# The second layer's latent norm: which engine takes the sums of squares, in what order, and when the root runs

## The reference

```python
def rmsnorm(x, w):
    return x * jax.lax.rsqrt(jnp.mean(x * x, axis=-1, keepdims=True) + EPS) * w
...
q = rmsnorm(hidden_states @ wq_a.T, q_a_ln_w) @ wq_b.T        # 192 latents for the queries
...
ckv = hidden_states @ wkv_a.T
kv = rmsnorm(ckv[..., :KV_LORA], kv_a_ln_w)                   # 64 latents for keys and values
k_pe = ckv[..., KV_LORA:][:, None, :, :]                      # 64 rotary columns, not normed
...
x1 = _bitlinear(x, w1)
x2 = _bitlinear(x, w2)
hidden = jax.nn.sigmoid(x1) * x2                              # the second layer's feed-forward
return _bitlinear(hidden, w3)
```

## Time and profile before

| What | Value |
|---|---|
| median of 3 runs | 1327.66 us (1326.15 to 1327.93) |
| profiled execution, its own time | 1328.96 us |
| its span | 1327.2 us |
| mean granted clock of TensorE over the span | 0.938 |
| first batch's block (d1b0) | about 523 to 585 us |
| second batch's block (d1b1) | about 585 to 653 us |

### The profile page before, as it was taken

How to read it: one execution, slowest core, us unless ns; L and a number is a source line. 1 busy time by engine, 2 the same in 40 slices (tenths; PEclk the granted TensorE clock), 3 DMA queues, 4 the chain that set the end, 5 groups by cost and what they waited for, 6 DMA issues and landing times.

```text
span 1327.2 us, 22453 instructions
## 1 busy us (share of the span) xinstructions
PE 1200.7 (90%) x7552; PEld 856.9 (65%) x7552; DVE 896.5 (68%) x2308; ACT 751.5 (57%) x1700; POOL 547.1 (41%) x567
## 2 busy tenths in 40 slices
PE   4888779999999889887799999999999999999898
PEld 3776744444443477776567776777777777777688
DVE  6867587899997344444577666677766667777743
ACT  2466216677776424545466656666665566666632
POOL 2435233444441100607065554556655445565310
PEclk9898756899998797888899999999999999999999
DMA  6773154454540284021211111110111121011315
GB/s 187 147 147 59 45 73 58 59 80 81 76 64 3 68 236 137 31 85 48 76 29 44 45 45 43 30 33 29 44 45 45 49 87 33 29 45 33 128 38 185
DMA packets 112466, 93.55 MB, mean 70 GB/s; under 512 B 49696, under 2 KB 102240, under 8 KB 110560
## 3 DMA queue, kind: packets, MB, share of 16 engines
q1 hardware_dynamic: 112352, 92.11, 29.6%
HBM read 53.02 MB, written 30.67 MB: 63 GB/s over the span
## 4 chain that ended last, share of the span: by engine, by line
PE 35%; DVE 11%; issue 3%; ACT 1%; DMA 0%; ACTq 0%; DVEq 0%
PE psum L1025 11%; PE psum L1073 9%; PE psum L194 8%; PE psum L1046 7%; DVE a_part L938 3%; DVE psum L943 3%; DVE a_pt L976 2%; DVE w L2289 1%; ACT a_p L990 1%; DVE w_lat L2289 1%; DVE q00l L2289 1%; DVE q01l L2289 1%; DVE a_nm L943 1%; DMA w<-wf_d 0%; DVE ql1l L2170 0%
## 5 line engine op out<-in xcount | busy, mean ns | idle before, releaser
L1007 POOL TENSOR_SCALAR a_p<-a_p,a_rl 128x128 f32<-128x128 f32 (+7 forms) x256 | 218.8, 856 | 307.5 <-DVE a_rl L949 307.5
L990 ACT ACTIVATE a_p<-psum,a_nm 128x128 f32<-128x128 f32 (+7 forms) x256 | 189.7, 741 | 55.7 <-DVE a_nm L943 54.1
L1508 ACT ACTIVATE a_pt<-psum 128x512 f32<-128x512 f32 (+3 forms) x384 | 167.9, 492 | 80.0 <-PE psum L1371 77.5
L1046 PE MATMUL psum<-ident,a_p 128*128 128x128 f32 x1152 | 175.4, 279 | 14.2 <-DVE a_pt L976 14.2
L976 DVE COPY a_pt<-psum 128x512 f32<-128x512 f32 (+1 forms) x192 | 114.5, 596 | 109.0 <-PE psum L1046 108.5
L974 ACT ACTIVATE a_pt<-psum 128x256 f32<-128x256 f32 (+2 forms) x192 | 87.5, 456 | 164.0 <-PE psum L1046 163.9
L1046 PEld LDWEIGHTS psum<-ident,a_p 128*128 128x128 f32 x1152 | 127.2, 140 | 62.3 <-issue 47.7
L1073 PE MATMUL psum<-a_pt,v 128*64 128x256 f32 (+1 forms) x1280 | 159.4, 370 | 1.4 <-ACT rows_k L1087 1.4
L1361 PE MATMUL psum<-a_op_k,a_op_q 64*128 64x512 f32 (+3 forms) x384 | 137.4, 456 | 9.1 <-ACT a_op_q L1527 8.1
L1371 PE MATMUL psum<-a_op_q,a_op_k 64*128 64x512 f32 (+3 forms) x384 | 132.6, 432 | 7.5 <-ACT a_pt L1508 6.2
L1371 PEld LDWEIGHTS psum<-a_op_q,a_op_k 64*128 64x128 f32 x384 | 65.1, 201 | 104.4 <-ACT a_pt L1508 88.4
(11 more groups left out here) (389 smaller groups left out, 2907.7 us busy)
## 6 DMA issues: line engine op xcount, KB each, us to landing
ot_d<-rows_k SPq DMA_DIRECT2D x16, 512.0 KB, 4.5
a_swap<-w_p SPq DMA_DIRECT2D x60, 128.0 KB, 2.3
rows_q<-qk_d SPq DMA_DIRECT2D x48, 128.0 KB, 4.5
rows_k<-qk_d SPq DMA_DIRECT2D x48, 128.0 KB, 7.5
w<-wf_d SPq DMA_DIRECT2D x15, 384.0 KB, 3.4
qk_d<-d_stage_h SPq DMA_DIRECT2D x64, 64.0 KB, 2.1
qk_d<-d_stage_l SPq DMA_DIRECT2D x64, 64.0 KB, 2.1
d_x<-in_L_attn_x_dram SPq DMA_DIRECT2D x8, 256.0 KB, 7.2
```

The costliest lines, as they stand in the source:

```text
L990: e.activation(s.p[:, t % NPB, 0:(i + 1) * P], C.score[t % 2][:, 0:(i + 1) * P], ACT.Exp, scale=-1.0, bias=s.nm[:, k:k + 1], accum_out=s.l ...
L1007: e.tensor_scalar(s.p[:, t % NPB, 0:(i + 1) * P], s.p[:, t % NPB, 0:(i + 1) * P], s.rl[:, k:k + 1], 1.0, ALU.mult, ALU.mult).then_inc(s.no ...
L1046: ins = e.transpose(C.turn[par][:, (k - k0) * P:(k - k0 + 1) * P], s.p[:, tt % NPB, k * P:(k + 1) * P], C.ident[:, :])
L1508: e.activation(pt[:, k // G0 % NPT, hd, off:HALF], bank_b("score", g, k)[:, off:HALF], ACT.Exp, scale=-1.0).then_inc(exped, 1)
```

## The change

`project1` gets an argument `squares_on`. In the first batch ("scalar") ACT still takes the squares, but those of tile tt-1 directly behind the copy of tile tt, in the part `first`. In the second batch ("vector") DVE takes them, with `tensor_tensor_reduce` in the part `rest`. The root stays in `rest` on ACT, which has nothing else now, and in the second block `rest` moves ahead of `lifts`.

```diff
-def project1(ph, C, W, cos, sin, kv_ln, xt_h, xt_l, ql_h, ql_l, keys, v):
+def project1(ph, C, W, cos, sin, kv_ln, xt_h, xt_l, ql_h, ql_l, keys, v, squares_on):
...
             e.activation(lat[:, tt, :], banks[tt % 4][:, 0:LAT], ACT.Copy).then_inc(lat_out, 1)
+            if squares_on == "scalar" and tt >= 1:
+                act_squares(e, tt - 1)
+        if squares_on == "scalar":
+            act_squares(e, NT - 1)
+
+    def act_squares(e, tt):
+        e.wait_ge(lat_out, tt + 1)
+        for n, cols in enumerate((slice(0, QL), slice(QL, E))):
+            e.activation(junk[:, tt, cols], lat[:, tt, cols], ACT.Square, accum_out=ms[:, n, tt:tt + 1]).then_inc(ssq, 1)
+
+    def dve_squares(e, tt):
+        e.wait_ge(lat_out, tt + 1)
+        for n, cols in enumerate((slice(0, QL), slice(QL, E))):
+            e.tensor_tensor_reduce(out=junk[:, tt, cols], in0=lat[:, tt, cols], in1=lat[:, tt, cols], scale=1.0, scalar=0.0,
+                                   op0=ALU.mult, op1=ALU.add, accum_out=ms[:, n, tt:tt + 1]).then_inc(ssq, 1)
 
     def scalar(e):
-        for tt in range(NT):
-            e.wait_ge(lat_out, tt + 1)
-            e.activation(junk[:, tt, 0:QL], lat[:, tt, 0:QL], ACT.Square, accum_out=ms[:, 0, tt:tt + 1]).then_inc(ssq, 1)
-            e.activation(junk[:, tt, QL:E], lat[:, tt, QL:E], ACT.Square, accum_out=ms[:, 1, tt:tt + 1]).then_inc(ssq, 1)
         e.wait_ge(means, 2)
         e.activation(ms[:, :, :], ms[:, :, :], ACT.Sqrt).then_inc(root, 1)
 
     def vector(e):
+        if squares_on == "vector":
+            for tt in range(NT):
+                dve_squares(e, tt)
         e.wait_ge(ssq, 2 * NT)
...
-                        run(nc, load, first, lifts, load_x(xb[1], source[1], came), rest, rotation, f, rotated, turn1(ph.part("t1b1"), C, rest, f))
+                        run(nc, load, first, rest, lifts, load_x(xb[1], source[1], came), rotation, f, rotated, turn1(ph.part("t1b1"), C, rest, f))
```

More of the change, by code:

```diff
@@ L2556, in program @@
                         loads = [load_x(xb[b], source[b], came[b]) for b in (1, 0)]
-                        first, rest = project1(ph.part("p1b0"), C, W, cos, sin, kv_ln, *xt[0], *ql[0], keys[0], v[0])
+                        first, rest = project1(ph.part("p1b0"), C, W, cos, sin, kv_ln, *xt[0], *ql[0], keys[0], v[0], "scalar")
                         f = feed1(ph.part("f1b0"), C, W, rest, 0, *xt[0], xb[0], came[0], acc_d,
@@ L2563, in program @@
                     with Phase(nc, "d1b1") as ph:
-                        first, rest = project1(ph.part("p1b1"), C, W, cos, sin, kv_ln, *xt[1], *ql[1], keys[1], v[1])
+                        first, rest = project1(ph.part("p1b1"), C, W, cos, sin, kv_ln, *xt[1], *ql[1], keys[1], v[1], "vector")
                         came = [ph.sem(f"x{n}_came") for n in range(NT // 2)]
```

## The result

| | before | changed |
|---|---|---|
| median of 20 runs, us | 1325.88 (1315.76 to 1329.45) | 1316.86 (1309.64 to 1331.69) |
| ratio to before | | 0.994 [0.9915, 0.9965] |
| profiled execution, its span | 1327.2 | 1308.7 |

The account below looks back on a forecast made before the run. The prediction took PE's waits to bound the kernel, here feed-forward's first restart waiting for the gate of job 0. Second batch -8.2 and first +1.5 made -6.7, 1322.3 us, or 1321.0 as a median; range 1318.0 to 1325.0.

Parts of the forecast that it names:

- The median of the runs shown is 1327.66 us, 1.3 below that execution, and the prediction is for medians: 1321.0 us: Whole kernel: -6.7 from the profiled 1328.96 gives 1322.3; lowered by 1.3 to the median's level, 1321.0 us.
- 1 us of scatter between runs: Whole kernel: margin added to the full-blocking case to set the range's upper end, 1325.0 us.
- -8.2: Second batch, PE's restart: 4.8 squares, 1.5 table load and root, 2.0 clock, less 0.1 late; bounds -8.3 to -7.5.
- I take three hits, 1.3: First batch: line 256, moved later, meets POOL's products three times at up to 0.44 each; part of +1.5, bounds -0.1 to +3.7.
- two tiles fit between two turns of POOL: First batch, line 256 on DVE beside POOL's products: the reason given for taking three hits, 1.3 us.
- The rival of full blocking: First batch: POOL and line 256 block each other fully, +3.7; second -7.5; total 1323.9 us; chance 0.17.
- whose cold clock stays as it is: First batch: PE's restart comes later by +1.5, with its cold clock unchanged.
- No turns: First batch: DVE and POOL take no turns, +0.2, with -8.3 in the second; total 1319.6 us; chance 0.1.
- A switch of tables at twice its load: Second batch, ACT: table switches cost twice their load, PE restarts 2.1 us later than forecast; 1323.0 us; chance 0.02.
- Squares slow enough to hold the root: Second batch: DVE's squares delay root and query copies; at 2.5 us a tile 1335.4 us; chance 0.03.
- Nothing moves: Second block: another wait behind the gate held it to the same end; 1327.7 us; chance 0.04.
- theory (E): Set up after the measurement: what lies beyond the sum comes from the clock in code that the change does not touch.

Follow-up runs that it names:

- e3_rows_late: Changed kernel, but DVE scales the eight rows of line 256 only behind its product for job HT1 + 1: 1312.05 us, 0.991 of before.
- e8_rows_late_again: Repeat of `e3_rows_late` with no edit, beside the changed kernel on the same chip: 1306.22 us, 0.9848 of before.
- e7_change_again: Repeat of the changed kernel with no edit: 1315.98 us, 0.9918 of before.
- e4_order_before: Changed kernel, but `rest` back behind `lifts` in the second block, squares still on DVE: 1323.87 us, 1.0034 of before.
- e1_first_only: Changed kernel, but the second batch has its old squares and old order, so only the first batch's change remains: 1325.29 us, 1.002 of before.
- e5_act_squares: Changed kernel with its new order, but the second batch's squares on ACT between its copies, as in the first batch: 1318.79 us, 0.9944 of before.
- e2_second_only: Changed kernel, but the first batch has its old squares on ACT, so only the second batch's change remains: 1317.44 us, 0.9968 of before.
- e6_pool_held: Changed kernel, but in the first batch POOL's first product waits until line 256 is through: 1310.76 us, 0.9877 of before.

## Why the prediction was wrong in the number and right in the direction

The median, 1316.86 us, lies 1.1 us below the range of 1318.0 to 1325.0 and 4.1 below the forecast of 1321.0. The difference from before was forecast as -6.7; measured are -8.0 [-11.3, -4.6] by the ratio, and -7.3 by the blocks of the traces. The steps:

- **"The median of the runs shown is 1327.66 us, 1.3 below that execution, and the prediction is for medians: 1321.0 us", and in the range "1 us of scatter between runs". This step failed.** Three runs within 1.8 us had me take the base for fixed. In 20 runs beside the changed kernel the same program had 1325.88, in the 35 of the next comparison 1323.92, from 1312.51 to 1335.86. From 1325.88 the sum gives 1319.2 and the range 1316.2 to 1323.2, which holds the median; 1.8 of the 4.1 us are this step. The stretch ahead of the blocks alone took 507.5 to 523.4 us.
- **Second batch, "-8.2": the mechanism and its terms right, one term missing.** The gate 6.3 earlier (6.33), no wait of ACT for DVE, PE's wait at 0.37 (said 0.4), the restart at 2.4 GHz (said so), the last pair on DVE 0.55 (said near 0.7, at most 0.86), POOL's wait of 5.4 gone. The block became 9.8 shorter and not 8.2: in the traces of the change 1.5 more came from the warm start of the block, which the sum did not have. Where the start was cold, in `e3_rows_late`, the block became 7.1 shorter, since there the clock fell once more, to 0.57 between 44 and 48 us into the block. The six traces with the whole second part have blocks of 58.0 (three times), 60.6, 60.7 and 61.0, in the mean 59.4: that is 8.4 shorter than before, and so the 9.8 of the two traces of the changed kernel are partly luck with the clock.
- **"I take three hits, 1.3": mis-sized.** By its own terms the root of the first batch moved like this: line 256 starts 9.20 after the memset instead of 7.89 (+1.3, said +1.5), takes 5.55 instead of 3.11 (+2.4, said +1.3), the wait for the squares falls away (-1.3, as said), and the means take 0.77 instead of 0.25 (+0.5, counted within the three hits). The root comes 2.9 later, and in the mean of all traces 2.3, where +1.5 was said. My reason, that two tiles fit between two turns of POOL, was false: once both run together one tile goes to each product of POOL and nearly every tile takes 0.88. The rival of full blocking (+3.7) had the mechanism; in this trace it came to 2.9, with five more long tiles instead of six and one long mean instead of two.
- **"whose cold clock stays as it is": right**, 0.50 behind the restart in both.
- The other rivals. No turns: refuted by 5.55 against 2.67. A switch of tables at twice its load: refuted, the load of 584.24 takes 1.28 and the root starts at 585.53. The prediction put this rival outside its range, yet its 1323.0 us lie inside 1318.0 to 1325.0; the time alone would not have told it apart. Squares slow enough to hold the root: refuted, the pair takes 0.55 where 1.7 was needed. Nothing moves: refuted, -7.3 us in the blocks.
- The rule of the Trainium skill (Vector Engine (DVE) Microarchitecture Reference, section Points that are easy to get wrong) that two sources in SBUF that are not bf16 halve the throughput of this family: the trace disagrees. 192 columns from SBUF took 0.36 us, just what the row with one operand in PSUM had given for that length; the estimate by the rule was 1.1 us a tile. Both sources were the same tile, and two different ones were not run; whether the instruction is of the form that the page means, no row says.
- The rule of the Trainium skill (GPSIMD Engine Reference, section Specifications) on interfaces to SBUF shared with VectorE: the trace agrees that the two engines hold each other up, 0.88 us a tile beside POOL's products and 0.41 with POOL held. Whether line 256 meets the page's condition (a two-port mode or two inputs from SBUF) no run shows.

**What stays open.** The ratio gives 8.0 us and that of the repetition 10.9, the medians 9.0 and 9.5, the blocks of the two traces 7.3. All lie within both intervals (4.6 to 11.3 and, in the repetition, 7.2 to 14.6), and no run tells whether more than the blocks is anything at all: theory (E) is neither shown nor refuted. It also stays open what makes the second block begin warm. The second batch's part can hardly be it, since all its instructions come behind that start, and one and the same kernel began cold in `e3_rows_late` and warm in `e8_rows_late_again`. Of the five traces with the changed kernel's first block three began the second warm (changed, `e7_change_again`, `e4_order_before`) and two cold (`e1_first_only`, `e5_act_squares`); of the four with the first block of before one did (`e2_second_only`). In all six warm traces the clock had fallen once late in the first block, to between 0.57 and 0.70 in a stretch of 4 us between 40 and 52 us behind its start; so it had in two of the six cold ones (before, `e5_act_squares`) and not in the other four. I have no mechanism for it, and the 1.5 us cannot be booked to the change.

**A better version.** `e8_rows_late_again`, the change with line 256 moved behind the feed-forward's middle, has 1306.22 us and 0.9848 [0.9813, 0.9883], below both kernels; on the same chip the changed kernel had 1315.98. The same kernel had 0.991 [0.9878, 0.9942] as `e3_rows_late`. Without it the first-batch part of the change costs 2.3 us at the gate: the root was held by work of DVE that is not needed until later in the block. Holding POOL (`e6_pool_held`) helps too, with the gate at 13.59 against 14.6 before. Line 256 late with the old squares was not run.

## What to carry to other kernels

Ask of every instruction that is moved what then ends the wait: taking squares off ACT bought nothing in the first batch, because the means stood behind eight tiles on DVE, and only 0.1 us in the second while they stood behind the query rests in DVE's list; the list of each engine has to be written out, not only that of the one relieved. Work that lands on another engine's busy stretch should be priced at full collision unless a row shows otherwise. And a base of three runs is a sample: compare the pieces between marks, and let the range hold the scatter of the clock.

## What the runs showed of the hardware that I had not expected

- **The scatter goes with the granted clock.** Of the 35 executions of the kernel before beside the first four runs, the shortest (1312.51 us) had a mean clock of 0.956 and the longest (1335.86) one of 0.935. From 150 to 230 us, in code that is the same, the kernel before (first row) and the changed one had:

```profile
150.00:230.00 80.00, 65.85 (x283) 39.23 (x287) 57.80 (x175) 29.17 (x56) 24.55 (x14) 0.62 0.45 64
```

```profile
150.00:230.00 80.00, 67.20 (x324) 39.83 (x323) 60.88 (x185) 30.03 (x60) 28.49 (x18) 0.69 0.46 64
```

  The second got 41 matmuls further in the same time. Over the whole stretch ahead the mean was 0.87 where it took 523 us and 0.91 where it took 507.5.
- **A stretch at 1.2 GHz can come and go behind the same instructions.** `e2_second_only` had none at its restart, but 44 us into the block, where PE had idled for 3.6 of 4 us; there it ran at 0.50, and its block is 3.0 us longer than that of the changed kernel, with the gate at the same 14.24. In the changed kernel PE idled for 3.1 of 4 us at the same place and came out at 1.00. The length of the gap does not settle it: in `e6_pool_held` PE idled for 3.1 of 4 us too, and ran at 0.50 behind it. The two stretches in `e2_second_only`, in the changed kernel, and in `e6_pool_held`:

```profile
619.78:623.78 4.00, 0.39 (x2) 0.00 (x0) 3.38 (x5) 2.25 (x4) 3.35 (x2) 0.86 0.00 0
623.78:627.78 4.00, 3.84 (x18) 3.88 (x19) 1.34 (x5) 1.61 (x2) 0.00 (x0) 0.50 0.40 133
```

```profile
616.81:620.81 4.00, 0.94 (x6) 0.55 (x5) 3.97 (x7) 3.13 (x5) 2.23 (x2) 1.00 0.00 0
620.81:624.81 4.00, 4.00 (x36) 4.00 (x34) 1.54 (x5) 0.73 (x1) 0.00 (x0) 1.00 0.41 135
```

```profile
608.29:612.29 4.00, 0.93 (x5) 0.54 (x4) 3.98 (x7) 3.15 (x5) 2.22 (x2) 0.83 0.00 0
612.29:616.29 4.00, 4.00 (x20) 4.00 (x20) 0.78 (x3) 0.71 (x1) 0.00 (x0) 0.50 0.41 135
```

- **DVE pays for nearly all of the turns.** A tile of DVE goes from 0.41 to 0.88 us; of POOL's products in the changed kernel the first takes 0.91, and those behind it 0.72 to 0.75. With POOL held (`e6_pool_held`) the first four take 0.73 or 0.74. Not every instruction of POOL does this to DVE: in `e3_rows_late` the same eight tiles ran beside POOL's scaling (`TENSOR_SCALAR`, 192 and 64 columns) and took 0.40 to 0.43, and it was POOL's that grew now and then, here from 0.43 to 0.58:

```profile
532.70 2.71 DVE L260 TENSOR_SCALAR rows_k<-rows_k,n_mv,n_rstd 128x256 f32<-128x256 f32 x8
```

```profile
533.71 0.58 POOL L1877 TENSOR_SCALAR p1b_qn<-p1b_lat,p1b_ms 128x192 f32<-128x192 f32 x1
```
